# Attention and experts on one core: x plus bias prepared in the prologue, two chunk buffers, early last x tiles, and the sums of P merged on Pool

## The reference

```python
def attn(ctx, latents, mask):                      # ctx 1601 x 192, latents 2048 x 256
    xn, ln = layernorm(ctx), layernorm(latents)
    q = ln @ Wq.T
    kv = concat([xn @ Wkv.T, ln @ Wlkv.T])         # keys from the context and from the latents
    k, v = split(kv)                               # 4 heads of 64
    attn = softmax(where(mask, rms(q) * SCALE @ rms(k).T, -max))
    return (attn @ v) @ Wo.T + bo
x = x + attn(ctx_768, layernorm(x), mask)
x = x + experts(layernorm(x))                      # softmax router, top 2 of 8, silu(gate) * up
```

## Time and profile before

| | us |
|---|---|
| median of 3 runs | 1138.31 (1138.18 to 1139.41) |
| the profiled execution | 1141.2 |
| its span | 1139.2 |
| TensorE busy | 983.2 (86%) |
| VectorE, ScalarE, Pool busy | 653.5, 477.6, 594.1 |
| chain that ended last: PE, POOL, issue | 47%, 20%, 10% |
| of it `acc_p` (L417) | 16% |

### The profile page before, as it was taken

The page is one execution under the profiler, slowest core; times in us unless marked ns, Lnnn a source line. Parts: engine busy times, 40 slices in busy tenths (PEclk is TensorE's granted clock), DMA queues, the critical chain, the costliest instruction groups (busy, mean ns, idle before and its releaser), DMA issues.

```text
span 1139.2 us, 15241 instructions
## 1 busy us (share of the span) xinstructions
PE 983.2 (86%) x4556; PEld 638.2 (56%) x4557; DVE 653.5 (57%) x1311; ACT 477.6 (42%) x751; POOL 594.1 (52%) x460
## 2 busy tenths in 40 slices
PE   2799779999999899898999999999882469999994
PEld 2565445555555555555554554555442458888883
DVE  3889776666666566566566566566125624444442
ACT  1456524455445446445455545454431022233231
POOL 4000018766974864854955855846820025556552
PEclk9899879999999999999999999999975579999998
DMA  6000002112111212121112212122169093332332
GB/s 173 1 1 1 9 5 72 54 56 70 61 61 65 71 55 70 57 69 65 61 61 70 65 56 75 56 65 75 56 262 367 16 360 48 54 51 51 51 52 27
DMA packets 66240, 85.15 MB, mean 75 GB/s; under 512 B 10283, under 2 KB 62444, under 8 KB 64140
## 3 DMA queue, kind: packets, MB, share of 16 engines
q1 hardware_dynamic: 49166, 56.57, 14.6%
q0 software_dynamic: 7488, 10.23, 5.5%
q10 hardware_dynamic: 9534, 17.70, 4.3%
HBM read 49.87 MB, written 34.60 MB: 74 GB/s over the span
## 4 chain that ended last, share of the span: by engine, by line
PE 47%; POOL 20%; issue 10%; ACT 8%; DVE 8%; DMA 5%; ACTq 2%; DVEq 0%; POOLq 0%; SPq 0%
POOL acc_p L417 16%; PE bPV L1249 10%; ACT PT L644 5%; PE bS L1238 4%; PE bM L1169 4%; POOL wraw L421 4%; PE bS L1239 3%; PE bA L1116 3%; DMA x2t<-x 2%; PE bG L1328 2%; DVE mpart L862 2%; PE bH L1345 2%; PE bV L1133 2%; PE bG L1330 1%; PE bG L1329 1%
## 5 line engine op out<-in xcount | busy, mean ns | idle before, releaser
L862 DVE TENSOR_REDUCE mpart<-bM 128x1 f32<-128x464 f32 x492 | 295.6, 635 | 178.8 <-PE bM L1169 177.6
L417 POOL TENSOR_TENSOR acc_p<-acc_p,PT 128x1024 f32<-128x1024 f32 x144 | 343.8, 2387 | 33.6 <-ACT PT L644 29.3
L644 ACT ACTIVATE PT<-bS 128x1024 f32<-128x1024 f32 (+1 forms) x240 | 232.2, 993 | 64.8 <-PE bS L1239 58.4
L1249 PE MATMUL bPV<-PT,V 128*64 128x512 f32 x928 | 233.1, 610 | 0.0
L1238 PE MATMUL bS<-Q,S 128*128 128x512 f32 x464 | 190.0, 409 | 3.8 <-ACT PT L644 1.5
L1169 PE MATMUL bM<-S,Q 128*128 128x464 f32 x492 | 175.1, 414 | 12.1 <-DVE mpart L862 7.0
L1239 PE MATMUL bS<-Q,S 128*128 128x512 f32 x464 | 183.9, 396 | 0.0
L417 POOL TENSOR_TENSOR acc_p<-PT 128x1024 f32<-128x1024 f32 x16 | 41.6, 2601 | 255.9 <-ACT PT L644 255.9
L615 ACT CAST whi<-wraw 128x256 fp32r<-128x256 f32 x96 | 38.9, 405 | 248.3 <-POOL wraw L421 245.1
L1169 PEld LDWEIGHTS bM<-S,Q 128*128 128x128 f32 x492 | 85.0, 191 | 97.4 <-DVE mpart L862 67.6
L1238 PEld LDWEIGHTS bS<-Q,S 128*128 128x128 f32 x464 | 88.2, 190 | 56.6 <-issue 22.7
(11 more groups left out here) (221 smaller groups left out, 1461.9 us busy)
## 6 DMA issues: line engine op xcount, KB each, us to landing
wraw<-w SPq DMA_DIRECT2D x96, 128.0 KB, 2.3
wsp_d<-whi SPq DMA_DIRECT2D x96, 128.0 KB, 2.2
wsp_d<-wraw SPq DMA_DIRECT2D x96, 128.0 KB, 1.7
W<-wsp_d ACTq DMA_DIRECT2D x8, 1536.0 KB, 18.9
W<-wsp_d SPq DMA_DIRECT2D x8, 1536.0 KB, 11.7
V<-x SPq DMA_DIRECT2D x1, 2048.0 KB, 12.8
x<-x ACTq DMA_DIRECT2D x12, 128.0 KB, 2.0
out<-x ACTq DMA_DIRECT2D x12, 128.0 KB, 1.9
```

What stands on the lines that cost most here:

```text
L417: pool.tensor_tensor(acc_p[:], one, PT[:, q % NPT, :, :], ALU.add).then_inc(sem("z_p"), 1)
L644: act.activation(PT[:, p % NPT, 0:n, :], bS[(w.h + p) % 2][:, 0:n, :], ACT.Exp).then_inc(sem("exp"), 1)
L862: dve.tensor_reduce(mpart[:, i, g:g + 1], banks[k % len(banks)][:, 0:PIECE], AX, ALU.max)\
L1249: last = pe.matmul(bPV[b * D:(b + 1) * D, 0, :], V[:, c, h * D:(h + 1) * D], PT[:, p % NPT, b, :], start=c < 2, stop=c >= NK - 2, skip_gro ...
```

## The change

- `z_merge` is done by Pool after its own adds of the unit, with the same waits; VectorE no longer has it. The sum into `acc_d[:, 0]` and the signal `zs` go with it.
- `whi` has two buffers. `w_hi(n)` waits for the subtraction of chunk n-2 and for the store of its own buffer's last high part.
- In the prologue Pool adds x and bias for all 16 tiles out of V into two buffers `xbs`, and SyncE stores them to `xb_d` in DRAM. ScalarE's copy of the values over such a tile waits for that add. `x_load` reads `xb_d` in place of x, and Pool's adds L432 and L441 are gone. The mask loop of Pool is written out.
- The last four x tiles are loaded by ScalarE in step 2 of the last unit, into a place under `QQ` (`Q1` and `Q2`, laid out by head parity) that is free by then. VectorE waits for them just before use, and waits for the stores of these rows (`ox_t`) before it writes G, which now lies over them.

```diff
+        QQ = sb("QQ", [P, 2, 2, QW], F32R, at=tq)
+        Q1, Q2 = QQ[:, :, 0, :], QQ[:, :, 1, :]
+        tq.close()
+        x2t = sb("x2t", [P, 2 * QB, DIM], at=t1)
...
-        whi = sb("whi", [P, WC], F32R, at=t1)
+        whi = sb("whi", [P, 2, WC], F32R, at=t1)
...
+            for t in range(NT):
+                sp.wait_ge(sem("xb"), t + 1)
+                sp.dma_start(xb[t, :, :], xbs[:, t % 2, :]).then_inc(sem(f"xb_st{t % 2}"), 16)
...
-            sp.wait_ge(sem("pv"), NP * UNITS)
-            for i in range(QB):
-                sp.dma_start(x2t[:, i, :], xt[NF + i, :, :]).then_inc(sem(f"xin_t{i}"), 16)
...
+            def x_bias(t):
+                if t >= 2:
+                    pool.wait_ge(sem(f"xb_st{t % 2}"), 16 * (t // 2))
+                pool.tensor_tensor(xbs[:, t % 2, :], V[:, NC + t, :], bob[:], ALU.add).then_inc(sem("xb"), 1)
+
+            pool.wait_ge(sem("c_bo"), 16)
+            for t in range(NC + 2):
+                k_mask(Step(None, t))
+                if t == 3:
+                    pool.wait_ge(sem("x_in"), 16)
+                if t >= 3:
+                    x_bias(t - 3)
+            for t in range(NC - 1, NT):
+                x_bias(t)
...
+            def z_merge(w):
+                pool.wait_ge(sem("z_p"), len(POOL_SUMS) * w.u + len(POOL_SUMS))
+                pool.wait_ge(sem("z_d"), len(DVE_SUMS) * w.u + len(DVE_SUMS))
+                pool.tensor_tensor(acc_d[:], acc_d[:], acc_p[:], ALU.add).then_inc(sem("zm"), 1)
+                pool.wait_ge(sem("zm"), w.u + 1)
+                pool.tensor_tensor(acc_d[:, 0, :], acc_d[:, 0, :], acc_d[:, 1, :], ALU.add).then_inc(sem("zs"), 1)
...
-                    if n == XB_AT and w.fin:
-                        pool.wait_ge(sem("xin"), 16 * w.tile + 16)
-                        pool.tensor_tensor(x2[:], x2[:], bob[:], ALU.add).then_inc(sem("xb"), 1)
+                z_merge(w)
...
-                pool.wait_ge(sem(f"xin_t{i}"), 16)
-                pool.tensor_tensor(x2t[:, i, :], x2t[:, i, :], bob[:], ALU.add).then_inc(sem("xb"), 1)
...
+                    if b == 'l':
+                        act.wait_ge(sem("xb"), t.back(NC).v + 1)
...
             def w_hi(n):
                 act.wait_ge(sem(f"raw{n % 2}"), 16 * (n // 2) + 16)
-                after(act, sem("wst_h"), 16 * n)
-                after(act, sem("wsplit"), n)
-                act.copy(whi[:], wraw[:, n % 2, :]).then_inc(sem("whi"), 1)
+                after(act, sem(f"wst_h{n % 2}"), 16 * (n // 2))
+                if n > 1:
+                    act.wait_ge(sem("wsplit"), n - 1)
+                act.copy(whi[:, n % 2, :], wraw[:, n % 2, :]).then_inc(sem("whi"), 1)
...
+            def x_load_last():
+                act.wait_ge(sem("s_mm"), NP * (UNITS - 1))
+                for i in range(QB):
+                    act.dma_start(x2t[:, i, :], xt[NT - QB + i, :, :]).then_inc(sem(f"xin_t{i}"), 16)
...
-                z_merge(w)
...
+                    dve.wait_ge(sem(f"xin_t{i}"), 16)
                     stats2(NF + i, x2t[:, i, :], bFY[i][:, 0, 0:DIM], st2t[:, i, :], mv2t[:, i, :])
...
+            dve.wait_ge(sem("ox_t"), 16 * QB)
             link(dve.tensor_tensor(G[:], flat.unsqueeze(2).to_broadcast([P, R, NBLK + 1]),
```

More of the change, by code:

```diff
@@ L110, in build @@
           router_t, w13, w2, out):
+    xb_d = nc.dram_tensor("xb_d", [TOK, DIM], F32, kind="Internal").ap()
     xln_d = nc.dram_tensor("xln_d", [TOK, DIM], F32, kind="Internal").ap()
@@ L191, in build @@
         qn = sb("qn", [P, 2, DIM], at=t0)
+        bob = sb("bob", [P, DIM], at=t0)
+        xbs = sb("xbs", [P, 2, DIM], at=t0)
         m_u8 = sb("m_u8", [P, NC], U8, at=t0)
@@ L206, in build @@
         t1 = ExitStack()
[L207 to L208 removed]
+        tq = ExitStack()
+        QQ = sb("QQ", [P, 2, 2, QW], F32R, at=tq)
+        Q1, Q2 = QQ[:, :, 0, :], QQ[:, :, 1, :]
+        tq.close()
+        x2t = sb("x2t", [P, 2 * QB, DIM], at=t1)
         PT = sb("PT", [P, NPT, 2, QW], at=t1)
@@ L216, in build @@
         t2 = ExitStack()
-        x2t = sb("x2t", [P, QB, DIM], at=t2)
         x3t = sb("x3t", [P, QB, DIM], at=t2)
@@ L329, in _ @@
                 sp.wait_ge(sem("whi"), n + 1)
-                sp.dma_start(wsp_d[e, 0, :, c:c + WC], whi[:].bitcast(F32)).then_inc(sem("wst_h"), 16)
+                sp.dma_start(wsp_d[e, 0, :, c:c + WC], whi[:, n % 2, :].bitcast(F32)).then_inc(sem(f"wst_h{n % 2}"), 16)
                 sp.wait_ge(sem("wsplit"), n + 1)
@@ L417, in z_sum @@
                 pool.tensor_tensor(acc_p[:], one, PT[:, q % NPT, :, :], ALU.add).then_inc(sem("z_p"), 1)
+            def z_merge(w):
[4 more added lines that the diff above has]
+                pool.tensor_tensor(acc_d[:, 0, :], acc_d[:, 0, :], acc_d[:, 1, :], ALU.add).then_inc(sem("zs"), 1)
             def w_lo(n):
                 pool.wait_ge(sem("whi"), n + 1)
-                pool.tensor_tensor(wraw[:, n % 2, :].bitcast(F32R), wraw[:, n % 2, :], whi[:].bitcast(F32),
+                pool.tensor_tensor(wraw[:, n % 2, :].bitcast(F32R), wraw[:, n % 2, :], whi[:, n % 2, :].bitcast(F32),
                                    ALU.subtract).then_inc(sem("wsplit"), 1)
@@ L648, in unit @@
                         x_load(w.tile)
+                    if p == 2 and w.last:
+                        x_load_last()
                     if p in SPLIT_AT:
@@ L661, in unit @@
                     c_row(v, w.next_h % 2)
+            for k in range(2):
+                act.wait_ge(sem(f"xb_st{k}"), 16 * NT // 2)
             q_hi(0, 0, 0)
@@ L666, in _ @@
             run_units(unit)
-            act.wait_ge(sem("wst_h"), 16 * E * NCH)
             for k in range(2):
+                act.wait_ge(sem(f"wst_h{k}"), 16 * E * NCH // 2)
                 act.wait_ge(sem(f"wst{k}"), 16 * E * NCH // 2)
@@ L894, in z_sum @@
                 dve.tensor_tensor(acc_d[:, 0:m, :], one, PT[:, q % NPT, 0:m, :], ALU.add).then_inc(sem("z_d"), 1)
-            def z_merge(w):
-                dve.wait_ge(sem("z_p"), len(POOL_SUMS) * w.u + len(POOL_SUMS))
-                dve.wait_ge(sem("z_d"), len(DVE_SUMS) * w.u + len(DVE_SUMS))
-                dve.tensor_tensor(acc_d[:], acc_d[:], acc_p[:], ALU.add).then_inc(sem("zm"), 1)
-                dve.wait_ge(sem("zm"), w.u + 1)
-                dve.tensor_tensor(acc_d[:, 0, :], acc_d[:, 0, :], acc_d[:, 1, :], ALU.add).then_inc(sem("zs"), 1)
             def stats2(t, x_, y, st, mv):
-                dve.wait_ge(sem("xb"), t + 1)
                 dve.wait_ge(sem("y_mm"), t + 1)
@@ L925, in unit @@
                     if p == Y_AT and w.fin:
+                        dve.wait_ge(sem("xin"), 16 * t + 16)
                         stats2(t, x2[:], bT[:, 0, 0:DIM], st2[:], mv2[:])
```

11 lines of the change are left out of this document (2 added, 9 removed).

## The result

The changed kernel takes 1100.31 us (median of 4 runs, 1100.04 to 1101.88) beside 1138.86 us (4 runs, 1138.18 to 1139.88) for the kernel before on the same chip. The ratio is 0.9664, interval 0.9647 to 0.968: 38.5 us faster. The forecast was 1096.5 with a range of 1088 to 1110; it is 3.8 us too low. The profiled execution took 1100.04 us, its span is 1098.3 us.

The account below looks back on a forecast made before the run. TensorE bounds the first units; later it waits, mostly on ScalarE copies behind single-buffered chunk copies. 28.8 us (stage) plus 13.0 (tail) makes 41.8; 1141.2 less 41.8 less 2.9 gives 1096.5 us, range 1088 to 1110.

Parts of the forecast that it names:

- the three waits: TensorE's waits in eleven later units: 11.0 us at the router matmul, 8.7 at the projection, 6.9 at x3's transpose.
- R1: Rival: chunk loads take their 5.5 us after all, copies stay late, only 8.4 + 13.0 us gained, 1117; chance 0.10.
- So I take all three as gone: Later units: copies move 2.2 us, longest single waits are under that, so 26.6 us go over eleven units.
- the exclusion between the two engines: At Pool's merge: two-SBUF-input VectorE instructions and GpSimd SBUF reads exclude each other; none met, a later merge risks 11 us.
- the last unit: Sixteenth unit: TensorE waits 4.79 us for x3; the copy ahead of the square root moves, gaining 2.2 us.
- the tail: After the last P·V: last x tiles loaded early without bias to add, logits' copy at 859.7 for 872.70, 13.0 us gained.
- R2: Rival: stores of x2 rows, queued while weights stream, hold VectorE's table G, 3.7 us lost, 1100; chance 0.10.
- the merge on Pool: End of each unit: Pool's two adds take 3.8 us, covered by its rest with 1.5 us to spare; cost nothing.
- R4: Rival: Pool's merge gets onto the path between units, delaying exp 4 and TensorE; up to 1157; chance 0.05.
- R3: Rival: the 4.9 us at score blocks and TensorE's whole last-unit wait go too, 7.5 us more, 1089; chance 0.13.
- The subtraction of 2.9 us: Whole kernel: the profiled execution lay 2.9 us above the median of three runs, so 2.9 came off the forecast.

Follow-up runs that it names:

- e1: Changed kernel with the old single `whi` buffer and its old waits, all else kept: 1119.91 us, ratio 0.9827 to the kernel before.
- e4: Kernel before with only x plus bias made in the prologue (one `whi`, merge on VectorE, last x tiles late): 1127.48 us, ratio 0.9892.
- e2: Changed kernel with the merge of the sums back on VectorE: 1099.85 us, ratio 0.9641 to the kernel before.
- e3: Changed kernel with the last four x tiles loaded by SyncE after the last P·V again: 1108.51 us, ratio 0.9723 to the kernel before.
- e7: Changed kernel with x + heads written to PSUM and copied to x2, late normalisation reading PSUM: 1098.89 us, ratio 0.9633 to the kernel before.
- e9: Changed kernel with x + heads in PSUM, late statistics behind step 8's maximum, then the copy to x2: 1090.07 us, ratio 0.9562 to the kernel before.
- e5: Kernel before run once more without edit, for a second profile: 1140.13 us against 1139.18, ratio 1.0007.
- e8: Changed kernel with late statistics behind step 8's maximum, last merge on VectorE, last copy of o ahead of ScalarE's W transfers: 1102.00 us, ratio 0.9674.
- e6: Changed kernel with `bn_stats` and `bn_aggr` of late units moved behind step 8's maximum: 1100.13 us, ratio 0.9657 to the kernel before.
- e10: e9 with last merge on VectorE, last copy of o ahead of W transfers, three experts' W early in place of four: 1091.49 us, ratio 0.957.

## Why the prediction was right, and where it was off

**Right: the three waits hang on the one buffer.** Units 1 to 3 kept their length, ten of the late ones became 2.1 to 2.4 us shorter and one 1.1 (forecast about 2.4), the chunk copies wait for their load, and less. e1 shows the split, 18.1 for the buffer and 6.3 for Pool's bias (6.0 in e4). R1 (the load no faster than the buffer was) came true in one unit of eleven only, where a store landed 3.8 us after its issue; it took 42.7 us in place of 41.4.

**Off by 2.2: "So I take all three as gone".** 24.4 in place of 26.6. Of the three waits 3.9 us stayed: 1.5 for the heads, in the one unit of R1, and 2.4 for x3. That the total is off by 2.2 only is in part luck: TensorE's busy time fell by 2.3 us, a term that the forecast did not have. For x3 a step failed. The comparison of each wait (up to 1.5 us) with the advance of ScalarE's copy (2.2 us said, 1.9 to 2.0 measured in unit 4) was sound for ScalarE's copies. It took VectorE's own time, 0.41 us for the normalisation, as fixed. But the chain of copy, square root and normalisation, freed from Pool's subtraction, moved into the Pool addition that it had followed before. e1 and e4, with one buffer, have the normalisation at 413 ns on average; the changed kernel, e2 and e3, with two, at 1084 to 1089; e7 at 544. The forecast did weigh the exclusion between the two engines, but looked for it only beside the moved merge, and only for instructions with two SBUF inputs.

**Off by 1.6: the last unit.** 0.6 in place of 2.2. The chunk copy ahead of the square root did move by about what was said: 26.5 us after the mark in place of 28.8, 2.3 earlier. From that copy to TensorE's transpose of x3 it then took 4.08 us in place of 2.81: the normalisation in between took 1.69 us in place of 0.41. That is 1.3 of the 1.6. With the normalisation short, in e7 and e9, the last unit takes 38.3 and 38.2 us. The rest is TensorE's way from the transpose to the next mark, 10.1 us in place of 9.7. That is scatter, since the kernel before has 9.7 and, in e5's profile, 10.1; it comes from the clock. TensorE's rows, changed kernel:

```profile
799.44 0.69 PE L1227 MATMUL bT<-ident,x 128*128 128x128 f32 x2 [5.21 <-DVE x L940]
800.06 3.68 PE L1274 MATMUL bPV<-PT,V 128*64 128x512 f32 x8
```

and e3, which differs only behind this place and in the four issues:

```profile
802.27 0.69 PE L1225 MATMUL bT<-ident,x 128*128 128x128 f32 x2 [5.24 <-DVE x L938]
802.89 3.06 PE L1272 MATMUL bPV<-PT,V 128*64 128x512 f32 x8
```

The idle time ahead is the same, and the eight matmuls take 3.68 and 3.06 us (1.94 where the clock is full). The granted clock, changed kernel from 802 and e3 from 805, in stretches of 2 us:

```profile
802.00:804.00 2.00, 2.00 (x7) 0.39 (x4) 0.00 (x0) 0.00 (x0) 1.58 (x3) 0.50 0.37 123
804.00:806.00 2.00, 2.00 (x9) 1.61 (x8) 0.00 (x0) 0.23 (x1) 0.00 (x0) 0.60 0.47 156
```

```profile
805.00:807.00 2.00, 2.00 (x10) 0.95 (x6) 0.00 (x0) 0.00 (x0) 1.41 (x3) 0.95 0.39 130
```

In e3 the clock was back 3 us after the restart, in the changed kernel only after about 6; that is the 1.5 us by which their last units differ (39.2 and 40.7). The loads that ScalarE issues in this unit do not show in it: the way from the transpose to the mark takes 9.0 to 10.1 us in the eight kernels that have them, and 8.6 to 10.1 in the four profiles without (the kernel before twice, e3, e4). What sets it stays open.

**Right: the tail.** 13.7 in place of 13.0. Pool's merge delayed TensorE's start by 0.37 us (0.3 said):

```profile
815.05 0.41 PE L1209 MATMUL bT<-twin,oT_a 128*128 128x64 f32 x2 [2.68 <-POOL acc_d L443]
```

Then the last sum of x2t and the logits' copy, beside the earlier trace rows:

```profile
827.59 0.41 DVE L930 TENSOR_TENSOR x2t<-x2t,bFY 128x256 f32<-128x256 f32 x1
...
831.47 0.19 DVE L993 COPY lg<-bL 128x32 f32<-128x32 f32 x1 [1.71 <-PE bL L1233]
```

From one to the other it takes 3.88 us where the forecast kept the old 5.11; that and a start 0.6 us later than said make the 0.7. R2 did not occur, by 0.3 us; e8 shows the price: at 3.3 us less it took 5.06.

**Right: the merge on Pool** costs nothing (e2), so R4 is out. At the end of unit 4 its two adds took 2.37 and 1.29 us (2.39 and 1.28 said), and Pool then rested 1.70 us ahead of its next add (1.5 said). R3 is out for this kernel, though e9 shows that its 4.9 us can be had when the normalisation is freed as well.

**The subtraction of 2.9 us** for the profile above its median was right: 2.5 of it was the prologue's scatter (e5), which the next profile did not have. Of the 3.8 us by which the forecast was low, 2.2 are the late units, 1.6 the last unit, 0.3 the end, less 0.7 in the tail, together 3.4; the rest is that 2.9 were taken off where the scatter gave 2.5. The range has a slip of its own: half way from 1096.5 to R1's 1117 is 1106.8, and not 1110; the measured time lies within either.

## To carry to other kernels

A wait that goes makes other work earlier, and that work can fall on an instruction that was short because its neighbour rested: check what each short instruction on the path will now run beside, here VectorE beside Pool. A wait can be what keeps two engines apart, as the wait for Pool's subtraction kept the normalisation behind Pool's addition. Where two small waits sit on one engine's order, moving either can hand the time to the other (e6, e7: nothing or 1.4 us); both together brought 10 us (e9). A large prefetch can hold small stores behind it, as here: once the path is shorter than the prefetch, shortening it further needs the prefetch moved, and that has its own price later (e8, e10).

## What the runs showed of the hardware

- An fp32 `tensor_scalar` of 128x256 from SBUF to SBUF takes 0.41 us alone and up to 1.69 us beside a Pool addition of 2.4 us (1.95 in e6); in the changed kernel each of ten ended 0.14 to 0.16 us after that addition. From PSUM to SBUF it takes 0.54 us in either case (e7, twelve of twelve within 6 ns).
- After some 5.2 us of idle time TensorE's clock stood at 0.50, the 1.2 GHz level, and came back about 3 us after the restart in e3 and about 6 us after it in the changed kernel, with the same work in between; 1.5 us of the unit hung on it.
- Small stores of 128 KB behind 1.5 MB transfers: issued at 825.98, the last of them held VectorE until 847.84 (e8); in the changed kernel the four took 15.1 us (median) to land, while an `out` store of that size in the kernel before landed in 5.1 us.
- Unit 0's mark came 2.2 us apart in two profiles of one and the same kernel (e5), as much as some of the effects looked for here.
